# Seven gathers at once, another end, and 56 unused tiny products on TensorE

## The reference

```
x = x + cross_attention(LN(x), ctx_1024, mask)     # 16 heads of 32, 257 keys a batch row
x = x + self_attention(LN(x))                      # 16 heads of 32, RMS norm on q and k, 32 keys
x = x + experts(LN(x))
# experts: m = 3-tap mix along the sequence; scores = tanh(m @ Wo1 + bo1) @ Wo2 + bo2
#          each token takes the expert of the highest score, of 9:
#          h = m @ W1[e] + b1[e];  y = h @ W2[e] + b2[e];  out = LN(z + y) * gamma + beta
```

## Time and profile before

| what | us |
|---|---|
| median of three runs | 752.23 (752.10 to 752.71) |
| the profiled execution's own time | 754.56 |
| its span, first to last instruction | 752.8 |
| TensorE busy in it | 710.5 (94%) |
| VectorE, ScalarE, GpSimd busy | 375.0, 339.9, 197.6 |

### The profile page before, as it was taken

One profiled execution on the slowest core, in us unless ns is written; L12 is line 12 of the kernel. 1 busy time (PEld: TensorE's weight loads), 2 busy tenths in 40 slices (PEclk: granted clock), 3 DMA queues, 4 the chain that ended last, 5 costly groups with the idle time before them and its releaser, 6 DMA issues. The chain is left out here.

```text
span 752.8 us, 20567 instructions
## 1 busy us (share of the span) xinstructions
PE 710.5 (94%) x8150; PEld 552.5 (73%) x8150; DVE 375.0 (50%) x993; ACT 339.9 (45%) x743; POOL 197.6 (26%) x281
## 2 busy tenths in 40 slices
PE   4999999999999999999999999998999889888994
PEld 3777787788778778778778778776787667674662
DVE  5545424424424334334443443676667775561665
ACT  4435535435444444443453444543354555342663
POOL 0001001001001000010010020147676776425755
PEclk9999999999999999999999999999999999788997
DMA  8211110110110110110011011240000105348830
GB/s 333 83 56 58 57 57 1 58 56 0 56 56 0 56 56 3 52 56 26 30 56 40 15 56 56 97 104 2 17 28 15 43 34 180 129 159 328 312 128 26
DMA packets 17557, 55.97 MB, mean 74 GB/s; under 512 B 6098, under 2 KB 6354, under 8 KB 14566
## 3 DMA queue, kind: packets, MB, share of 16 engines
q1 hardware_dynamic: 13926, 40.64, 15.8%
q0 software_dynamic: 3584, 14.69, 5.3%
HBM read 46.93 MB, written 10.49 MB: 76 GB/s over the span
## 5 line engine op out<-in xcount | busy, mean ns | idle before, releaser
L96 PE MATMUL pj<-W_both 128*128 128x512 f32 x544 | 221.7, 407 | 9.9 <-DVE W_both L595 9.9
L98 PE MATMUL pj<-W_both 128*128 128x512 f32 x544 | 213.4, 392 | 0.0
L97 PE MATMUL pj<-W_both 128*128 128x512 f32 x544 | 212.5, 391 | 0.0
L96 PEld LDWEIGHTS pj<-W_both 128*128 128x128 f32 x544 | 102.6, 189 | 43.1 <-issue 23.5
L98 PEld LDWEIGHTS pj<-W_both 128*128 128x128 f32 x544 | 102.5, 188 | 22.8
L236 POOL COPY q_b<-Q_T 128x128 f32 (+1 forms) x32 | 9.3, 291 | 415.2 <-PE tp L359 349.0
L97 PEld LDWEIGHTS pj<-W_both 128*128 128x128 f32 x544 | 102.8, 189 | 19.0
L493 ACT ACTIVATE K<-pj,bk 128x512 f32<-128x512 f32 x64 | 44.2, 691 | 135.6 <-PE pj L98 135.6
L654 DVE CUSTOM_DVE_ANT_0 m_flat<-sc,mask 128x257 f32<-128x257 f32 x64 | 24.7, 424 | 116.3 <-PE tp L359 95.0
L508 ACT ACTIVATE p_flat<-m_flat,nmax 128x257 f32<-128x257 f32 x128 | 63.8, 500 | 25.5 <-DVE nmax L654 25.4
L500 ACT ACTIVATE V<-pj 128x512 f32<-128x512 f32 x64 | 38.2, 597 | 73.3 <-PE pj L98 72.1
(11 more groups left out here) (365 smaller groups left out, 1155.8 us busy)
## 6 DMA issues: line engine op xcount, KB each, us to landing
raw<-ctx_dram SPq DMA_DIRECT2D x15, 1024.0 KB, 4.7
experts<-w_dram SPq DMA_DIRECT2D x6, 768.0 KB, 5.8
raw<-w_dram SPq DMA_DIRECT2D x4, 1024.0 KB, 4.9
x_nat<-x_dram SPq DMA_DIRECT2D x2, 1024.0 KB, 11.9
rows<-z3s SPq DMA_DIRECT2D x8, 256.0 KB, 2.0
rows<-x_nat SPq DMA_DIRECT2D x8, 256.0 KB, 2.8
rows<-xm SPq DMA_DIRECT2D x8, 256.0 KB, 2.9
raw<-wk_dram SPq DMA_DIRECT2D x2, 512.0 KB, 5.6
```

The lines of the kernel that those rows point to most:

```text
L96: eng.matmul(out, a_hi, b_hi, start=first, stop=False)
L97: eng.matmul(out, a_lo, b_hi, start=False, stop=False)
L98: return eng.matmul(out, a_hi, b_lo, start=False, stop=last)
```

## The change

Three things, all in the second block. First, GpSimd starts seven gathers at once; the eighth, ninth and tenth each wait until TensorE has done the transposes of the second, third and fourth slot. Second, the end is reordered: on VectorE `residual(15)` comes before `centre(14)`, on GpSimd the last two roots come between the scatters 13 and 14, and SyncE instead of GpSimd waits for the scatters to land. Third, TensorE gets 56 products of 32 x 32 weights with one column, whose result is overwritten, before `out_proj` of step 6, the first step behind the loop.

```diff
-        AHEAD = 10
+        AT_ONCE, LANDINGS = 7, 10
...
-        slot_in = [sem(f"slot_in{i}") for i in range(AHEAD)]
+        slot_in = [sem(f"slot_in{i}") for i in range(LANDINGS)]
...
             eng.dma_start(gamma, row_on_all(io["gamma"])).then_inc(ex_in, 16)
+            for i in range(NH):
+                eng.wait_ge(stored[i], len(range(i, NS, NH)) * 16)
...
-            for k in range(AHEAD):
+            for k in range(AT_ONCE):
                 gather(k)
-            for k in range(NS):
+            for k in range(AT_ONCE, LANDINGS):
+                eng.wait_ge(xT_done, k - AT_ONCE + 2)
+                gather(k)
+            for k in range(NS - 2):
                 make_root(k)
                 if k:
                     scatter(k - 1)
-                if k + AHEAD < NS:
-                    gather(k + AHEAD)
+                if k + LANDINGS < NS:
+                    gather(k + LANDINGS)
+            scatter(NS - 3)
+            make_root(NS - 2)
+            make_root(NS - 1)
+            scatter(NS - 2)
             scatter(NS - 1)
-            for i in range(NH):
-                eng.wait_ge(stored[i], len(range(i, NS, NH)) * 16)
...
+            def idle_tiles(n):
+
+                for _ in range(n):
+                    eng.matmul(pw[1][0:HD, 0:1], ident[0:HD, 0:HD], ident[0:HD, 0:1], start=True, stop=True)
+
             def out_proj(it):
...
+                if isinstance(it, int) and it == NT - LEAD:
+                    idle_tiles(56)
                 project(pw[1][:, :], o2_hi, o2_lo, 4).then_inc(proj_done, 1)
...
-            for k in range(NS - 1):
+            for k in range(NS - 2):
                 residual(k)
                 centre(k)
                 if k:
                     finish(k - 1)
+            residual(NS - 2)
+            finish(NS - 3)
             residual(NS - 1)
-            finish(NS - 2)
-            centre(NS - 1)
-            finish(NS - 1)
+            for k in range(NS - 2, NS):
+                centre(k)
+                finish(k)
```

## The result

The changed kernel takes 761.25 us (758.99 to 762.12, 4 runs), the kernel before 752.47 us (752.10 to 753.21, 4 runs) beside it: a ratio of 1.0106 [1.0084, 1.0128], so 1.1% slower. The forecast was 751.2 us, with a range of 746.6 to 754.5: wrong in sign and outside the range. The execution profiled took 758.99 us, with a span of 757.3 us.

What follows compares the result with a forecast made beforehand. TensorE, busy 94% of the span, was taken as the bound. Span 752.8 + 2.6 (products) - 1.9 (shift) + 0 (gathers) - 1.7 (end) = 751.8; the -1.0 difference applied to the median gave 751.2 us, range 746.6 to 754.5.

Steps and rivals of the forecast that it cites:

- What the holds are: TensorE's "issue" waits behind the loop are code arriving late at edges of 256-instruction blocks: 0.80, 0.45 and 2.14 us.
- The products' own time: Before step 6's projection, 112 pairs at 27 ns cost 3.0 us; bounds 0.9 and 12, upper one kept at 6.
- The upper bound: For the tiny products' price: 6 us (54 ns a pair) kept instead of 12, since load time follows the columns.
- The cover of 0.4 us: TensorE's slack of 0.36 us before the second group of transposes hides 0.4 of the tiny products' 3.0 us.
- the slower rival: Tiny products let TensorE's clock fall: their last third +1.0, step 6's projection +2.0, so 754.2 us; chance 0.19.
- two rivals: Holds vanish and clock stays up (746.7 us, 0.16); tiny products cost the clock (754.2 us, 0.19).
- The shift: 224 more instructions move block edges behind step 6: gate -0.45, last scores -1.1, step 7 -0.3; -1.9 us, bounds -3.4, +1.6.
- the early case (1.2): Last scores: next code packet starts 1.2 us on, nothing left of 2.14; if as late as now, hold 2.0; half taken.
- the three known holds: TensorE behind the loop: 0.80 us in step 7's scores, 0.45 in the gate, 2.14 in the last scores.
- The gathers: GpSimd's tenth gather up to 4 us late, hidden since its slot is transposed some 20 us later: 0, upper bound +1.
- The rival of the hole: Spacing the gathers closes the hole among the first slots: -2.8 us, so 748.4 us; chance 0.24.
- The end: Last scatter 0.5 us sooner, GpSimd's drain 1.2 us gained by beginning before the landing: -1.7 us, bounds -2.2 and 0.

Runs made afterwards that it cites:

- the increments: Changed kernel with 224 (or 112) semaphore increments on TensorE ahead of step 6's projection waits instead of the 56 products: 787.95 us, 1.0449 (112: 765.63 us, 1.0162).
- second profile: Profile of the changed kernel run once more, unchanged: 760.54 us, 1.0071 to the kernel before.
- the wide ones: Changed kernel with each of the 56 unused products made of 128 x 128 weights and 64 columns: 778.22 us, 1.0324 to the kernel before.
- N: Changed kernel without its 56 unused products, so seven gathers and the new end only: 751.75 us, 0.9983 to the kernel before.
- the new end alone: Kernel before with only the reordered end, ten gathers at once and no unused products: 752.53 us, 0.9980 to the kernel before.

## Why the prediction was wrong, step by step

- **What the holds are: right.** I counted along TensorE's instruction list from the end of self-attention's loop, and added what a kernel has put in at the start. Between that loop and the slots, every hold of over 0.4 us without a producer (the increments themselves aside) then begins on the same place within a block of 256, in the kernel before and in the experiments, whatever was put in (one further in the two kernels where a wait was moved behind the products). The breaks moved as counted: after 101 products, 117 with 56 unused ones, 101 with 64. The size of a block shows in the transfers of the kernel before: between the holds that end at 611.22 and 647.27, 1280 instructions apart, the code queue moved five packets of together 0.08 MB, so 256 instructions and 16 KB each, and some 64 bytes an instruction:

```profile
q8 instruction: 5, 0.08, 1.0%
```

- **The products' own time: too small.** 3.0 us were forecast; it is 3.98 us in the profile after (5.37 - 1.39) and 5.54 us in the second one. At the full clock a pair takes 32 ns, not 27, and the pairs behind the fall of the clock take 53 to 54 ns. The upper bound had load time follow the columns, and the pairs do so roughly: 32 ns with 32 columns of weights, 0.12 us with 128 (the wide ones, ahead of the fall). The cover of 0.4 us was right: the second group of transposes follows the first without a wait in both profiles.
- **The clock: a step left at nothing, which the slower rival had.** The projection of step 6 takes 5.49 us in place of 3.07, +2.4 us, where that rival gave +2.0, and +1.0 for the products' last third, where the traces give 0.4 to 2. The clock fell within the products, as that rival had it, but behind 98 of the 112 in the first profile and not ahead of the last third. At 0.5 a product takes somewhat less than the twice as long that two rivals took: the wide products start 0.43 us apart in place of 0.23, 1.8 times. What made me give it 0.19 was that I set the price of idling and of empty work side by side without a row of either; the wait of 1.41 us alone leaves the clock at 1.0 in the kernel before, the wait and the products together don't.
- **The shift: the step that failed.** Forecast -1.9 us with bounds of -3.4 and +1.6. The same 224 instructions at the start cost 1.0021 - 0.9983 = 0.38%, 2.9 us, but by the two intervals that may be 0.4 to 5.4 us, and it takes in the stretch ahead of the loop, 1.2 us longer in the trace (68.5 - 67.3), which the change leaves in place. From the transposes ahead of step 6 on, the traces say 2.4 us (165.7 - 163.3). In the changed kernel's own tail, 8.6 us longer than N's, what is left over from products, cover and clock is 2.6 us, and 2.1 us in the second profile. So the shift costs some 2.4 us where it was to save 1.9.

  The gate's 0.45 us went as forecast (without products it is 0.16 us in one trace), and step 7's hold shrank as forecast in one profile (0.80 to 0.48 us; 0.71 in the second). The last scores kept 1.83 us where I took half of 2.14: the packet started 3.0 us after the block ahead of it was entered, between the early case (1.2) and the late one.

  And I looked only at where the three known holds went, not at the edges that had been harmless. The one behind the last scores, in the last weighted sum, became the worst: 2.83 us. With the 56 at the start the holds behind the loop sum to 4.6 us, without products to 2.8, so they make 1.8 of the 2.4 us. Between 584 and 700 us the clock is also at 0.5 for 23.9 us, against 17.0 without products. That this makes the rest is not shown.
- **Why that one.** The last scores hold TensorE till 651.23, and then it enters the next block. In the changed kernel's transfers there is no packet of code between 651.3 and 657.8; the next one comes just behind, and the code runs 2.2 us after its start:

```profile
q8 instruction: 1, 0.02, 2.5%
```

  That is the whole of the code queue from 657.8 to 660.2. So this block's packet starts some 6.7 us after the block ahead of it is entered, as one did in the kernel before (6.8 us). I had seen such delays, and treated them as belonging to two places instead of as something that any edge can have. What delays them is open. Other transfers fill most of the five microseconds before it here, but none did in the kernel before.
- **The gathers: 0 forecast, 0 measured** (-0.4 us, interval -1.7 to +1.0). The rival of the hole was right in that the hole closes, and wrong in its worth of 2.8 us. That the gathers close it isn't shown, since it is closed with ten gathers and the products as well.
- **The end: right in its sum, not in its parts.** -1.7 us forecast, -1.5 us by the ratio and -1.0 us in the traces. The drain's part was taken as 1.2 and is 1.4 us. The last scatter was to come 0.5 us sooner and ends 0.4 us later behind TensorE's last product (6.53 against 6.14 us).
- **Edges that cost nothing.** The sum for "slower" has a term for this case, a third of a rival's 0.12. No run shows the term: the three holds of the kernel before sum to 3.39 us, and with the products in the wait at the start, shifts of 112 and 224 instructions lie 5.9 us apart (749.13 and 754.99 us).

The sum with the measured terms: 4.0 to 5.5 for the products, -0.4 for their cover, 2.4 for the clock behind, 2.4 for the shift, -1.5 and -0.4 for the end and the gathers: +6.5 to +8.0 us. The ratios give +8.0 us for the change and +5.3 us for its repetition. With the repetition's own products (5.5) the sum is +8.0, where its ratio's interval ends at +7.3; the execution profiled was the slowest of its six (763.12 us). So the terms are good to a microsecond or two, no better. Of the 10 us between forecast and result, the shift makes 4.3, and products and clock 3.8 to 5.3.

## What to carry to other kernels

TensorE's long unrolled stream is fetched in blocks of 16 KB here, 256 instructions, and what the insertion did behind itself was as large as its own cost (2.4 us by the shift and 2.4 by the clock, against 4.0): count every block edge behind it, those that are harmless today too, and take the latest packet seen anywhere as the bound for each (here 6.8 us after the block ahead was entered). To shift code, put the filler where the engine waits anyhow and its clock doesn't matter, such as ahead of the first weights: there 20 to 28 unused products gained 3 to 4 us against N, while 56 lost 3 and 40 lost 5. And before pricing an edit on such an engine, run it once padded: a gain or loss of some 0.5% may be its place in the code alone, as these were (0.4 to 0.7%).

## What the runs showed of the hardware

- A semaphore increment on TensorE cost 0.15 us in a row of 224, more than four times a load and product of 32 x 32 by one column (0.032 us).
- Every filler at step 6 let the granted clock fall from 1.0 to 0.5: small products, 128 x 128 by 64 columns (0.21 us a pair with the clock at 0.5, 0.12 us ahead of the fall), and an array left idle by increments (at 0.5 for 34.1 us with 224). It came back only after wide products had begun: after 6.8 us in the changed kernel, 10.2 us in its second profile and 3.4 us with 28 products.
- Unused products stayed costly past themselves: the projection behind them takes 5.49 us in place of 3.07. The clock fell at another point in each of two profiles of one kernel, and the products take 3.98 us in one and 5.54 in the other.
- Code ran 2.2 to 2.7 us after its packet started, as the ends of the holds show (657.9 to 660.15 in the changed kernel, 608.5 to 611.22 before). Of the 15 packets behind the loop in the changed kernel, nine start 0.4 to 1.4 us after the block ahead is entered, the others 1.9 to 6.7 us after.
- GpSimd's drain behind indirect DMAs ended 2.7 us after the last of them ended on GpSimd where nothing waits for the landings ahead of it (the changed kernel, N, the new end alone); with that wait, in the kernel before, it ended 4.05 us after.
